# A 3x3 convolution in f16 on Trainium2: the left and right taps read their plane, and write PSUM, column by column

## The reference

```python
# layer 1: a 3x3 convolution whose weights are a mixture of 4 experts, chosen per image
out = conv(_gn(x), w_experts)                 # 4 x 128 output channels, 3x3, padding 1
out = einsum('beohw,be->bohw', out, routing)  # routing: sigmoid of a small product per image
x = x + silu(batchnorm(out))
# layer 2: a 3x3 convolution with weights of -1, 0 or 1
Wb = jnp.sign(W)
x = x + conv(_gn(x), Wb)                      # 128 -> 128 channels, 3x3, padding 1
```

## Time and profile before

| | us |
|---|---|
| median of 2 runs | 280.63 (279.56 to 281.71) |
| the profiled execution, its own time | 279.12 |
| its span, first to last instruction | 277.3 |
| PE busy in it | 270.6 (98%) |
| DVE busy | 245.5 (89%) |
| ACT busy | 208.5 (75%) |

### The profile page before, as it was taken

The page is one execution under the profiler, slowest core; times in us unless marked ns, Lnnn a source line. Parts: engine busy times, 40 slices in busy tenths (PEclk is TensorE's granted clock), DMA queues, the critical chain, the costliest instruction groups (busy, mean ns, idle before and its releaser), DMA issues.

```text
span 277.3 us, 4016 instructions
## 1 busy us (share of the span) xinstructions
PE 270.6 (98%) x1324; PEld 185.7 (67%) x1324; DVE 245.5 (89%) x439; ACT 208.5 (75%) x421; POOL 52.5 (19%) x59
## 2 busy tenths in 40 slices
PE   7999899999999999999999999999999999999996
PEld 6644756759586776859576775858576675848554
DVE  4898989999999999999999999999999999992732
ACT  3597788886988788787979788796978885727750
POOL 2001011214111031414123041414113041212000
PEclk9999999999999999999999999999999999999999
DMA  7999925442635445362635544371554545460422
GB/s 229 391 381 325 274 118 147 77 99 67 118 103 95 132 79 132 51 120 79 113 113 78 151 74 105 68 136 76 95 135 76 152 58 96 103 125 2 76 76 78
DMA packets 11397, 34.68 MB, mean 125 GB/s; under 512 B 1264, under 2 KB 3568, under 8 KB 11376
## 3 DMA queue, kind: packets, MB, share of 16 engines
q0 software_dynamic: 4032, 14.68, 31.3%
q1 hardware_dynamic: 7056, 19.47, 19.1%
q10 hardware_dynamic: 288, 0.26, 0.3%
HBM read 11.34 MB, written 15.73 MB: 98 GB/s over the span
## 4 chain that ended last, share of the span: by engine, by line
PE 88%; ACT 4%; DVE 3%; issue 1%; DMA 1%; POOL 1%; SPq 0%; ACTq 0%; DVEq 0%
PE pc L474 40%; PE pb L439 14%; PE pa L439 13%; PE pe_ L439 12%; PE pd L429 6%; DMA X<-x 1%; PE ps L410 1%; PE ps L405 1%; PE pb L474 1%; PE ps L414 1%; ACT y L738 1%; POOL rstd L352 1%; DVE U L932 0%; ACT hn L754 0%; DVE lo L1044 0%
## 5 line engine op out<-in xcount | busy, mean ns | idle before, releaser
L474 PE MATMUL pc<-lo,ws 128*128 128x496 f16 (+5 forms) x288 | 64.7, 371 | 0.0
L932 DVE SCALAR_TENSOR_TENSOR U<-we,route,U 128x1152 f32<-128x1152 f32 x45 | 63.5, 1410 | 0.1
L474 PE MATMUL pc<-hi,ws 128*128 128x496 f16 (+5 forms) x288 | 62.8, 372 | 0.0
L352 POOL TENSOR_TENSOR rstd<-ve,nhalf 128x2 f32<-128x2 f32 (+1 forms) x19 | 26.4, 1391 | 136.5 <-ACT ve L663 136.5
L474 PEld LDWEIGHTS pc<-hi,ws 128*128 128x128 f16 x288 | 28.1, 98 | 30.8 <-issue 0.3
L474 PEld LDWEIGHTS pc<-lo,ws 128*128 128x128 f16 x288 | 28.4, 105 | 25.5
L439 PE MATMUL pa<-V,UM 128*128 128x256 f32 (+1 forms) x180 | 41.8, 382 | 0.0
L439 PE MATMUL pb<-V,UM 128*128 128x256 f32 (+1 forms) x180 | 40.6, 375 | 0.1
L439 PE MATMUL pe_<-V,U 128*128 128x256 f32 (+1 forms) x180 | 40.6, 375 | 0.0
L439 PEld LDWEIGHTS pb<-V,UM 128*128 128x128 f32 x180 | 34.1, 190 | 5.7 <-issue 0.8
L439 PEld LDWEIGHTS pe_<-V,U 128*128 128x128 f32 x180 | 34.1, 190 | 3.8
(11 more groups left out here) (110 smaller groups left out, 387.2 us busy)
## 6 DMA issues: line engine op xcount, KB each, us to landing
X<-x SPq DMA_DIRECT2D x15, 512.0 KB, 5.2
out<-X SPq DMA_DIRECT2D x14, 512.0 KB, 2.6
X<-y POOLq DMA_DIRECT2D x14, 512.0 KB, 4.5
out<-ev POOLq DMA_DIRECT2D x14, 512.0 KB, 5.5
we<-w_experts SPq DMA_DIRECT2D x3, 768.0 KB, 8.2
out<-X SPq DMA_DIRECT2D x3, 256.0 KB, 2.0
ws_raw<-w_sign SPq DMA_DIRECT2D x1, 576.0 KB, 10.9
X<-x ACTq DMA_DIRECT2D x2, 128.0 KB, 3.0
```

The lines of the kernel that those rows point to most:

```text
L352: g.tensor_tensor(rstd[:, c, a:b], ve[:, c, a:b], nhalf[:, a:b], ALU.pow).then_inc(rstd_ready, 1)
L474: mm = mm_(rows[:, r0 - first // W:r1 - first // W, c0:c1], ws[:, tap * C:(tap + 1) * C], (hi, lo)[part][i % 2][:, r0 + ky - 1:r1 + ky - 1 ...
L932: v.scalar_tensor_tensor(out=flat(U[i % RING][:]), in0=flat(we[:, e, :, :]), scalar=route[:, i, e:e + 1], in1=flat(U[i % RING][:]), op0=AL ...
```

## The change

In `product`, the output and the plane are the same boxes of rows and columns as before. Where the tap is a left or right one (kx = 0 or 2), both are now walked with the rows innermost: the first 16 (or 15, 8, 7) elements are those of one column, then comes the next column. Products and sums are the same, as are the weights, the order of the taps and every semaphore. Middle taps are as before.

```diff
-                rows = conv_psum(first, last).rearrange("p (h w) -> p h w", w=W)
-                mm = mm_(rows[:, r0 - first // W:r1 - first // W, c0:c1], ws[:, tap * C:(tap + 1) * C],
-                         (hi, lo)[part][i % 2][:, r0 + ky - 1:r1 + ky - 1, c0 + kx - 1:c1 + kx - 1],
+                to = conv_psum(first, last).rearrange("p (h w) -> p h w", w=W)[:, r0 - first // W:r1 - first // W, c0:c1]
+                plane = (hi, lo)[part][i % 2][:, r0 + ky - 1:r1 + ky - 1, c0 + kx - 1:c1 + kx - 1]
+                if kx != 1:
+                    to, plane = to.rearrange("p h w -> p w h"), plane.rearrange("p h w -> p w h")
+                mm = mm_(to, ws[:, tap * C:(tap + 1) * C], plane,
                          start=(part == 0 and tap == TAP_ORDER[0]), stop=(part == 1 and tap == TAP_ORDER[-1]))
```

## The result

The changed kernel takes 509.68 us (median of 2 runs, 508.89 to 510.47) where the kernel before takes 280.63. The ratio is 1.820, with a 95% interval from 1.808 to 1.831. It is much slower, as forecast, but the forecast was 354.5 us with a range up to 431. The time fell on the case that had 0.08: two steps a column, worked out at 511 us.

The account below looks back on a forecast made before the run. PE was taken to bound the kernel: 279.12 us profiled + 75.1 for slower edge taps - 1.2 of waits = 353.0, plus 1.5 to the runs' median, 354.5 us. Likeliest range 346 to 361 us; 8-in-10 range up to 431.

Parts of the forecast that it names:

- What bounds the kernel: Whole kernel: PE sets the end, 88% of the chain; in the steady part a slower tap moves the end one for one.
- The count and the bookkeeping: Second convolution's edge taps: 1.174 us lost a half, four halves an image, 75.1 us in all, less 1.2 us of waits.
- the waits that go: PE's waits in image 0 (0.8 us) and the last stretch (0.4 us) vanish behind slower taps: 1.2 us back.
- 70%: Sign in the profile after: DVE's share of busy time falls from 89% to about 70%, with new waits on PE.
- its reason, that f32 taps keep it up: Against the rival of a clock fall to 1.2 GHz (some 515 us, chance 0.02): f32 taps at half rate keep the clock.
- The value I take: Turned f16 edge taps: one column a step, 0.416 us for 16 x 31, 1.174 us lost a half; chance 0.72.
- A jump costs two steps: Rival for turned edge taps: each far element needs a second step, 0.83 and 0.78 us a tap, 511 us; chance 0.08.
- a case between: Rival for turned edge taps: a column costs 1.5 steps, 0.62 us for 16 x 31, 431 us; chance 0.08.
- the two cases above it: Rivals: two steps a column, 511 us, chance 0.08; granted clock falls to 1.2 GHz, some 515 us, chance 0.02.
- The lower bound: Rival of no loss: turned edge taps cost 0.209 us, only odd runs waste; 0.9 us back, 279.7 us; chance 0.10.

Follow-up runs that it names:

- experiment 10: Against the changed kernel: only the right taps (kx = 2) turned, left taps as before the change; 394.14 us, ratio 1.408 to the kernel before.
- experiment 1: Against the changed kernel: edge taps still read the plane column by column but write PSUM in one run; 568.37 us, ratio 2.027 to the kernel before.
- Experiment 2: Against the changed kernel: edge taps still write PSUM column by column but read the plane in one run; 353.5 us, ratio 1.262 to the kernel before.
- experiment 3: Against the changed kernel: in images 1 to 14 edge taps read at steps of 2 to 64 elements, writing PSUM in one run; 491.77 us.
- experiment 5: Against the changed kernel: in images 1 to 14 edge taps read runs of 2 to 16 neighbours, 32 elements apart, writing PSUM in one run; 296.71 us.
- experiment 7: Against the changed kernel: in images 1 to 14 edge taps read runs of 4 at six offsets within 16 bytes, writing PSUM in one run; 290.54 us.
- experiment 11: Against the changed kernel: all edge taps read and write one run instead of rows of 31; ratio 0.996 to the kernel before.
- experiment 9: Against the changed kernel: edge taps read column by column but write PSUM with a step of 2 columns within one run; 505.12 us.

## Why the prediction was wrong

**What bounds the kernel: right.** PE held 88% of the chain, nothing hid a slower tap, and the loss is the taps' sum: half of the taps, half of the loss (experiment 10).

**The count and the bookkeeping: right.** 64 halves, four taps of 16 rows and two of 15, and the waits that go. Put the measured 3.61 us a half in the place of 1.174 and the sum gives 510 us; the run gave 509.7. The f32 blocks stayed as the text said, and so did the middle taps but for 0.02 us that they start late. DVE's busy share fell to 49%, not 70%, because the span is so much longer. The clock stayed too, but its reason, that f32 taps keep it up, did not secure that: with the same slow reads and neighbours written it fell (experiment 1). That it held is luck as far as the text goes.

**The step that failed** is "The value I take: ... each takes its own step, and the f16 tap goes at the rate of one column a step", with 0.416 us a tap. Measured: 0.81 to 0.83. The f32 rows of the same shape were the nearest rows by size and by number of columns, but not by what the change changed: they read neighbours. (They are also but one of the two rows that an f32 matmul has, which the text did not see; the price was meant for one step a column, so the sum does not hang on it.) Experiment 2 shows what 0.416 is the price of, the write side, where the text's mechanism holds: 353.5 us. The read side was taken to work likewise, and it does not. It is charged by lines of 16 bytes, two steps for each at the least, and a step of 32 elements touches a line for each column (experiments 3, 5 and 7). The dearer side alone is paid: 0.81 to 0.83 us a tap with both turned, as with the reads alone.

**The rival "A jump costs two steps"** had the right price, 511 us, and the right place. I gave it 0.08 on this argument: "the jump at the end of each row of 31 costs the f32 taps nothing". The argument is void. A row of f32 is 31 elements of 4 bytes, so nearly every line there gives four columns and takes four steps for them, more than its least two; a jump to a new line is dear only when less than two steps of work are taken from it. One jump in 31 says nothing of 31 in 31. Nor is the jump itself what costs, as the rival has it: rows of 4 neighbours with a jump behind each are free (experiment 5).

**What the pages said.** The page "SBUF — State Buffer" of the Trainium skill, Specifications (TRN2), wants two hits on each 16-byte line, and charges for each crossing. The runs bear out the line and the two hits, with a size that the page does not give: two steps a line at the least, four times the f16 price for single elements. A crossing as such costs nothing here: runs of 16 cross a line's end and jump, and take 0.215 us like whole rows. The text put it down as a rule without a row, gave it the direction, and left its size to a rival with little chance. The page "PSUM — Partial Sum Buffer" of the Trainium skill, Specifications (TRN2), says that any non-contiguous pattern slows matmuls. The measurements differ, and they decide: runs of 2 with jumps are free (0.216 us), single columns of an f16 product cost double, runs of 3 are charged as 4 (0.256 us for 480 columns), and single columns of an f32 product cost nothing.

**The range.** It had one step a column and a case between, up to 431, and left out the two cases above it with 0.10 together. Both bounds of the unknown price, 0.209 and 0.83 us a tap, stood in the text; no row spoke for one over the other, and the range should have reached to both.

**The lower bound** was right in its reason, odd runs (experiment 11), and could not come about: turning the tap makes the inner run of most of them even (16 rows), but each of its elements single.

## What to carry to other kernels

In these runs a matmul's time was set by its two patterns, apart from its number of columns. For the moving operand (the one that is read column after column, here the plane), count the 16-byte lines it touches: at least two steps of 0.84 ns for each, so a short run should not lie across a line's end. For an f16 product's output, count pairs of neighbours. The dearer side is paid. Walk both with the innermost dimension in one piece of an even length. If another order is needed, blocks of 4 f16 elements that begin on 8 bytes are as good as whole rows to within 0.02 us a tap. And when a change turns a pattern that no row of the trace shows, a row of the same shape in another pattern is no estimate: measure the one tap first.

## What was not expected of the hardware

- A read step of 2 f16 elements is free to within 0.01 us: 0.22 us for 512 columns (experiment 3).
- Read steps of 16 and 32 bytes are a little dearer than those of 64 and 128, 0.88 and 0.91 us against 0.84 and 0.86. Why was not tried, and counting lines does not give it.
- The first slow tap behind a quick one is short by 0.02 to 0.04 us, and the next quick one is late by as much.
- The granted clock fell to 1.2 GHz for about two thirds of the time in all four runs with slow reads and neighbours written to PSUM (mean 0.665), and partly in the read ladder (0.774), but not with slow reads and single columns written (1.000 in the changed kernel and in experiment 9), at the same pace of the taps. With only the right taps slow it stayed up. What the chip goes by in this is open; that it costs 59 us of 568 is measured.
- The edge taps that read column by column take hardly longer at 1.2 GHz than at 2.4: 0.83 to 0.84 us against 0.81 to 0.83 (experiment 1), while a whole row takes 0.40 for 0.22. So the price of a line on the read side did not stretch with the granted clock.
